# A recommender tower on one core: the fold of Wl ahead of the layers' weights, and 12 of 26 features normalized by ScalarE

## What is computed

```python
e = stack([tbl_f[ids[:, f]] for f in range(26)], axis=1)      # 2048 x 26 x 64
x = layer_norm(dense @ Wd.T, gd, bd)                          # 2048 x 128
y = layer_norm(einsum('bnd,ed->bne', e, Ws), gs, bs)          # each feature to 128 numbers
y = einsum('bne,pn->bep', y, Wsi)                             # 26 features to 32
y = layer_norm(y, gsi, bsi)
T = concatenate([x[:, None, :], swapaxes(y, 1, 2)], axis=1)   # 33 vectors of 128
Z = einsum('bnd,bmd->bnm', T, T)                              # pairwise products
out = layer_norm(Z[:, tril] @ Wl.T, gl, bl) * mask            # 384 of 512 kept
h = relu(concatenate([out, dense], axis=1) @ W_top1 + b_top1)
h = relu(h @ W_top2 + b_top2)
y = h @ W_top3                                                # 2048 x 1
```

## Time and profile before

| | |
|---|---|
| three runs, median (lowest to highest) | 621.14 us (621.01 to 622.87) |
| the profiled execution, in all | 624.07 us |
| its span | 621.9 us |
| TensorE busy, and its mean granted clock | 522.8 us (84%), 0.948 |
| VectorE busy | 518.9 us (83%) |
| ScalarE busy | 295.7 us (48%) |
| GpSimd busy | 403.4 us (65%) |
| gathers on GpSimd | 416, first at 3.14 us, last at 536.09 us |

### The profile page before, as it was taken

How to read it: one execution, slowest core, us unless ns; L and a number is a source line. 1 busy time by engine, 2 the same in 40 slices (tenths; PEclk the granted TensorE clock), 3 DMA queues, 4 the chain that set the end, 5 groups by cost and what they waited for, 6 DMA issues and landing times.

```text
span 621.9 us, 17561 instructions
## 1 busy us (share of the span) xinstructions
PE 522.8 (84%) x6955; PEld 390.4 (63%) x6955; DVE 518.9 (83%) x1073; ACT 295.7 (48%) x730; POOL 403.4 (65%) x422
## 2 busy tenths in 40 slices
PE   1462777689999999999999999999899899988886
PEld 1352555547676767676767676676767577756566
DVE  3499689999999999999998989898989789996610
ACT  0410243545555546464645465555546364635422
POOL 6777775777777777777777777777777777400000
PEclk9955877899999999999999999999999899998999
DMA  7311111111111111111111121111111111100000
GB/s 181 104 25 33 27 29 30 27 35 27 35 29 35 28 37 28 36 27 27 38 27 36 27 38 28 35 29 37 27 38 28 27 27 27 20 1 2 1 1 2
DMA packets 22609, 20.22 MB, mean 33 GB/s; under 512 B 12016, under 2 KB 14720, under 8 KB 22528
## 3 DMA queue, kind: packets, MB, share of 16 engines
q0 software_dynamic: 13312, 13.66, 12.3%
q1 hardware_dynamic: 8400, 4.33, 2.7%
q10 hardware_dynamic: 816, 1.11, 0.6%
HBM read 19.07 MB, written 0.01 MB: 31 GB/s over the span
## 4 chain that ended last, share of the span: by engine, by line
PE 41%; DVE 21%; issue 15%; POOL 9%; ACT 8%; DMA 4%; SPq 2%; ACTq 0%; DVEq 0%; POOLq 0%
POOL emb L255 9%; PE b_y L342 7%; PE b_l L397 7%; PE b_l L414 6%; PE b_l L423 5%; PE b_z L354 4%; DVE nrm L774 3%; DVE V L807 3%; DMA emb<-in_tbl,idx 3%; PE b_mix L330 3%; ACT mixed L501 3%; PE b_a L312 2%; DVE yb L789 2%; DVE byn L784 2%; PE b_a L321 2%
## 5 line engine op out<-in xcount | busy, mean ns | idle before, releaser
L255 POOL DMA_INDIRECT emb<-in_tbl,idx x416 | 402.7, 968 | 132.8 <-issue 117.6
L506 ACT ACTIVATE sq<-yb 128x1024 f32<-128x1024 f32 x64 | 67.7, 1057 | 154.8 <-DVE yb L789 154.8
L789 DVE TENSOR_TENSOR yb<-b_y,bias_y 128x1024 f32<-128x1024 f32 x64 | 78.1, 1220 | 20.3 <-PE b_y L342 19.8
L342 PE MATMUL b_y<-mixed,projw 64*128 64x512 f32 x256 | 74.0, 655 | 24.2 <-ACT mixed L501 24.1
L807 DVE TENSOR_TENSOR V<-yb,rstd_y 128x256 f32<-128x256 f32 x256 | 91.9, 422 | 2.2
L796 DVE TENSOR_REDUCE var_y<-sq 128x32 f32<-128x1024 f32 x64 | 77.8, 1216 | 7.0 <-ACT sq L506 5.6
L397 PE MATMUL b_l<-wlt,zt 128*128 128x512 f32 x160 | 72.9, 602 | 0.8 <-issue 0.8
L330 PE MATMUL b_mix<-mix,byn 128*128 128x128 f32 x512 | 72.3, 287 | 0.0
L321 PE MATMUL b_a<-gram_w,embt 128*128 128x128 f32 x416 | 64.7, 298 | 6.0 <-ACT embt L490 5.2
L490 ACT ACTIVATE embt<-b_a 128x512 f32<-128x512 f32 (+1 forms) x64 | 33.0, 516 | 76.6 <-PE b_a L312 76.5
L354 PEld LDWEIGHTS b_z<-V 128*32 128x32 f32 x4096 | 46.0, 111 | 34.5 <-issue 17.8
(11 more groups left out here) (131 smaller groups left out, 686.8 us busy)
## 6 DMA issues: line engine op xcount, KB each, us to landing
emb<-in_tbl,idx POOLq DMA_INDIRECT x416, 2.5
dense<-in_r_dense_t SPq DMA_DIRECT2D x16, 128.0 KB, 2.2
V<-in_L_rec_Wl ACTq DMA_DIRECT2D x1, 1056.0 KB, 5.2
w<-in_W_top SPq DMA_DIRECT2D x2, 512.0 KB, 6.4
w<-in_W_top SPq DMA_DIRECT2D x1, 768.0 KB, 5.3
out_y<-y_sb SPq DMA_DIRECT2D x16, 0.5 KB
idx<-in_ids SPq DMA_DIRECT2D x1, 195.0 KB, 5.1
wd<-in_L_rec_Wd SPq DMA_DIRECT2D x1, 128.0 KB
```

The costliest lines, as they stand in the source:

```text
L255: pool.indirect_dma_start(out=emb[t % 2][:, f, :], out_offset=None, in_=tables[f], in_offset=bass.IndirectOffsetOnAxis(ap=idx[:, t, f:f + ...
L342: last = nc.tensor.matmul(b_y[:, j2, :], projw[r, :], mixed[c % 2][r, :], start=True, stop=True, tile_position=(64 * j2, 0))
L789: nc.vector.tensor_tensor(yb[c % 2][:, :, :, :].rearrange("e h s p -> e (h s) p"), b_y[:, :, :].rearrange("e h (s p) -> e (h s) p", p=NP), ...
```

## The change

Three things change.

1. W_top1's last two blocks count for `w_mlp` and no longer for `w_x`, and are loaded ahead of W_top2. SyncE waits for `w_wl` ahead of the eight loads of `w_mlp`.
2. Wl's preparation lies earlier: `prepare_wsq` in quarter 0 (ahead of the first variance), `fold` in 1 and 2, `prepare_mlp` and `fold_sums` in 3, `prepare_gain` in 4, `prepare_wlt` in 5 to 9.
3. ScalarE normalizes features 0 to 11, each with one activation with the reciprocal as its scale, in four pieces: 0 to 3 at the end of quarter 4t+3, and in quarter 4t+4 features 4 to 6 ahead of its square, 7 to 9 behind it, and 10 and 11 at the end. VectorE keeps features 12 and 13 of the first half and the second half. A new semaphore `act_nrm` counts the pieces; the shuffle, VectorE's next first half and GpSimd's first batch of a tile wait for it.

```diff
+ACT_FEATURES = 12
+ACT_PIECES = 4
...
-        N_REC, N_X, N_MLP, N_WL = 4, 4, 7, 3
+        N_REC, N_X, N_MLP, N_WL = 4, 3, 8, 3
...
             load(dense[1][:, :], dense_v[1], dense_loaded[1])
+
+            sp.wait_ge(w_wl, 16 * N_WL)
             load(b2[:, :], a["b_top2"].rearrange("(c p) -> p c", p=P), w_mlp, True)
...
+            load(w1[:, 3:5, :], a["W_top1"][MAXD:, :].rearrange("(c p) m -> p c m", p=P), w_mlp)
             load(w2[:, :, :], a["W_top2"].rearrange("(c p) m -> p c m", p=P), w_mlp)
-            load(w1[:, 3:5, :], a["W_top1"][MAXD:, :].rearrange("(c p) m -> p c m", p=P), w_x)
...
                     after(pool, nrm_ready, 2 * (t - 2) + b // 2 + 1)
+                    if b == 0:
+                        after(pool, act_nrm, ACT_PIECES * (t - 1))
...
-                if h == 6:
+                if h == 4:
                     prepare_gain()
-                if 6 <= h < 6 + RC:
-                    prepare_wlt(h - 6)
+                if 5 <= h < 5 + RC:
+                    prepare_wlt(h - 5)
...
+            def normalize(t, lo, hi):
+
+                act.wait_ge(rstdn_done, 2 * t + 1)
+                after(act, byn_ready, 2 * t)
+                for f in range(lo, hi):
+                    last = nc.scalar.activation(nrm[:, :, f], emb[t % 2][:, f, :], ACT.Copy, scale=rstd_n[:, f:f + 1])
+                last.then_inc(act_nrm, 1)
...
+                if (t := tile(h, DENSE_NORM + 1)) is not None:
+                    normalize(t, 4, 7)
...
+                if (t := tile(h, DENSE_NORM + 1)) is not None:
+                    normalize(t, 7, 10)
...
+                if (t := tile(h, DENSE_NORM + 1)) is not None:
+                    normalize(t, 10, 12)
+                if (t := tile(h, DENSE_NORM)) is not None:
+                    normalize(t, 0, 4)
-                if h == 1:
+                if h == 0:
                     prepare_wsq()
...
+                if k == 0:
+                    after(dve, act_nrm, ACT_PIECES * t)
...
-                for f in range(f0, f0 + n, 2):
+                for f in range(max(f0, ACT_FEATURES), f0 + n, 2):
...
                 dve.wait_ge(nrm_ready, 2 * (t + 1))
+                dve.wait_ge(act_nrm, ACT_PIECES * (t + 1))
...
-                if h == 1:
+                if h == 0:
                     prepare_wsq()
-                if h in (2, 3):
-                    fold(h - 2)
-                if h == 4:
+                if h in (1, 2):
+                    fold(h - 1)
+                if h == 3:
                     prepare_mlp()
                     fold_sums()
-                if h == 6:
+                if h == 4:
                     prepare_gain()
-                if 6 <= h < 6 + RC:
-                    prepare_wlt(h - 6)
+                if 5 <= h < 5 + RC:
+                    prepare_wlt(h - 5)
```

More of the change, by code:

```diff
@@ L151, in tower @@
         emb_transposed, embt_copied, gw_done = sem("emb_transposed"), sem("embt_copied"), sem("gw_done")
-        prod_done, varn_done, varm_done, stdn_done, rstdn_done, nrm_ready, byn_ready = (
-            sem("prod_done"), sem("varn_done"), sem("varm_done"), sem("stdn_done"), sem("rstdn_done"), sem("nrm_ready"), sem("byn_ready"))
+        prod_done, varn_done, varm_done, stdn_done, rstdn_done, nrm_ready, act_nrm, byn_ready = (
+            sem("prod_done"), sem("varn_done"), sem("varm_done"), sem("stdn_done"), sem("rstdn_done"), sem("nrm_ready"), sem("act_nrm"), sem("byn_ready"))
         mix_done, mixed_copied, proj_done = sem("mix_done"), sem("mixed_copied"), sem("proj_done")
```

## The result

The changed kernel takes 616.49 us (median of 13 runs, 614.14 to 620.67) beside 622.15 us of the kernel before (13 runs, 619.49 to 625.28). The ratio is 0.9905 with a 95% interval of 0.9887 to 0.9923; times the 621.14 us from above that is 615.2 us, where 615.4 was forecast. It is faster, by 5.7 us. The profiled execution took 615.92 us, its span is 614.1 us (621.9 before), and TensorE's mean granted clock 0.98 (0.948 before). The two clocks are not to be compared: in the start-up this profile shows 1.00 where the matmuls were as slow as before.

The account below looks back on a forecast made before the run. The prediction took GpSimd's gathers as the bound, saturated for 396 us. Removing 4.7 us of its waits and 1.0 us of end lag gives -5.7 us, from 621.14 to 615.4 us; range 612.3 to 618.8.

Parts of the forecast that it names:

- The bound: From 141 us to its last gather GpSimd never waits: saturated for 396 us, at 1.27 us a gather.
- The sum: Over the whole span, GpSimd's vanished waits and less lag at the end give -5.7 us, 621.9 to 616.2.
- -4.7 (waits): GpSimd's real waits for the gram, up to about 141 us, all vanish: 4.7 us, bounds 0 and 4.7.
- -1.0 (lag): Compute behind the gathers at the end: 2.0 us before, 1.0 taken as gained through VectorE's lighter load.
- rival 2: TensorE's clock falls after gather waits: 618 to 622.7 us, about 642 if every tile is hit (under 0.01); 0.11 with another rival.
- The shift that survives is 3.5 us: Start-up: transposes behind the 40th gather, at 61.44 us, can come only 3.5 us earlier, when its data is there.
- It is not on GpSimd's path: VectorE losing 6 of 13 normalizations a tile, 1.5 us a tile, 24 us in all, doesn't delay GpSimd.
- It makes the compute about 30.8 us a tile: VectorE's relief makes compute 30.8 us a tile against GpSimd's 32.8, winning back lag at 2 us a tile, not 0.5.
- Up to 3.6 us a tile: ScalarE's 12 added activations a tile, 302 ns each, cost up to 3.6 us, hidden in its idle time; taken at nothing.
- The rule on the shared port: If VectorE's instructions with two SBUF inputs slow gathers, fewer normalizations save 1.9 us: 613.5 us, left out of the sum.
- the rival's share for nrm: Freer gathers as nrm partly leaves VectorE: 24 of 143.6 us leave, saving 1.9 us; 612.5 to 613.5 us, chance 0.11.
- The rivals on the other side: No earlier start, 620 to 621 us (0.11 with the cold-clock rival); or ScalarE's pieces slow tiles, about 640 us (0.04).

Follow-up runs that it names:

- normalization alone: The changed kernel with loads, copies, folds and Wl's transposition where they were before; ScalarE still normalizes features 0 to 11: 618.14 us beside 621.93, ratio 0.9934.
- start-up part alone: The changed kernel with all 26 features normalized on VectorE again, keeping the changed loads and Wl's earlier preparation: 618.5 us beside 622.87, ratio 0.9933.

## Why the prediction was right, and where its steps were wrong

**The bound: right.** GpSimd's gathers set the time. Where its waits are gone the kernel is 5.7 us shorter, and with 22 gathers a tile it is shorter still, until GpSimd waits again. It is a bound by a narrow margin: 64 gathers fewer, 81 us of GpSimd's time, gave only some 9 us.

**The sum: right in its total, and in its terms only in part.** Forecast for the span was -4.7 (waits) and -1.0 (lag) = -5.7. Measured in the profiled execution: -4.7 waits, -2.2 gathers' own time, -2.1 lag, +1.2 drain = -7.8 (621.9 to 614.1). The medians moved by 5.7. One execution against another thus moved 2 us more than the medians; the execution of before was 2.9 us above the median shown first, so a match to the tenth is partly luck. The scalings that left VectorE are 21.6 us (51.7 to 30.1), not 24. And in rival 2 the sum is wrong: 31 us on top of 615.4 are 646, not 642.

**"The shift that survives is 3.5 us": undersized.** The transposes behind the 40th gather came at 56.22 instead of 61.44, so 5.2 us earlier: that gather ended at 54.6 and not 55.4, and they followed 1.6 us behind it, where I had put the 2.5 us of a usual landing. First shuffle 51.87, forecast 53 or earlier; the last gather started at 529.25, forecast near 531.4. The matmuls of wd came at 10.49, forecast 10.1 to 10.5, and the first batch at 18.92, the late end of the 15.7 to 19 forecast: its last landing took 5.9 us while the weights were loading.

**"It is not on GpSimd's path": wrong in the start-up tiles.** The prediction did add 1.5 us each for tile 0's and the next tile's lighter normalization, but it called VectorE's relief worth only the lag at the end, and the expectations took it that without the start-up part GpSimd's pauses would stay. The normalization alone removes all of GpSimd's waits, the start-up part alone 3.1 of 4.7, and each has a ratio of 0.993; together 0.9905. Both draw on the same 4.7 us, so their gains can't add in full. I had read VectorE's share from the steady tiles and not looked at the tiles from 57 to 157 us, where TensorE has less to do and VectorE is nearly full, in one of them 32.79 of 33.57 us. That either part still adds something to the other is likely but not firm: the intervals are 0.9912 to 0.9955 (start-up part) and 0.991 to 0.9958 (normalization) alone and 0.9887 to 0.9923 together, and they overlap. In the traces with the normalization alone and with both, the 2.6 us of span between them are 1.6 from the gathers, 1.9 from a lag that is a matter of when the cold tile falls, and -1.0 from the drain.

**"It makes the compute about 30.8 us a tile": wrong.** It is 32.15; TensorE's 30.3 us of work and its waits for ScalarE are most of that, and I take them for what sets it. After the cold tile the lag fell by 0.5 to 0.6 us a tile, not by 2. I subtracted VectorE's 1.5 us from a tile that TensorE, at 84% over the span but 94% in these tiles (121.18 of 128.60), was setting. So the lag of 0 at the end isn't VectorE's work: the cold tile fell at tile 7 instead of 14, and eight tiles were left to recover. With the normalization alone it fell at tile 14 again and 1.8 us of lag remained; with the start-up part alone, VectorE at its full load, no tile was cold and no lag remained.

**"Up to 3.6 us a tile" for ScalarE: right in size, and hidden as argued.** By their records the 192 activations took 402 ns in the mean, beside a nearest row of 302; but in a row they overlap, and the group is busy 55.8 us, 0.29 each or 3.5 us a tile. ScalarE keeps 136 us of idle time ahead of its squares. VectorE's reciprocals of the sample side, which wait for ScalarE's root, stood idle 31.2 us; before it was 18.9 us, so part of what VectorE was freed of came back as waiting for ScalarE, on an engine with time to spare.

**The rule on the shared port: half borne out, not settled.** The gathers' mean fell from 968 to 963 ns, 2.2 us in all, close to the 1.9 worked out. By 5.3 ns it just passed the 5 that the prediction had named as a sign of being wrong. But the start-up part alone, with all scalings on VectorE, has 968, the normalization alone, with VectorE as light as in the changed kernel, has 967, and the changed kernel with 22 gathers has 973. The mean doesn't follow nrm. The single gathers in the trace of the kernel before say more: of the 56 that took over 1.0 us, 42 ran beside an instruction that writes `V`, as 93 of all 416 did, and only 10 beside one of nrm, as 62 of all did. So the slow gathers go mostly with V, which stays, and the rival's share for nrm had little ground; what lowered the mean stays open. The Trainium skill ("GPSIMD Engine Reference", Key points) names instructions with two SBUF inputs as what contends with GpSimd; both groups are such, and the trace bears it out for V and not for nrm. Why they differ no run shows.

**The cold TensorE: limited itself, as argued.** One tile in a run is made longer by over 3 us: 36.37 us (tile 14) before, 36.47 (tile 7) after, 35.77 (tile 14) with the normalization alone, none with the start-up part alone. Three stretches of 4 us of the changed kernel, each behind a wait of TensorE for a gather, and one of three tiles in which such waits are short:

```profile
114.14:118.14 4.00, 4.00 (x22) 3.69 (x24) 3.96 (x4) 1.94 (x4) 3.02 (x4) 0.65 0.14 25
147.40:245.79 98.39, 90.77 (x1289) 67.46 (x1287) 86.63 (x162) 61.69 (x165) 74.62 (x79) 1.00 0.17 32
247.30:251.30 4.00, 3.98 (x22) 3.74 (x24) 3.82 (x7) 1.95 (x4) 3.08 (x4) 0.64 0.16 32
81.30:85.30 4.00, 3.96 (x22) 3.84 (x22) 3.93 (x10) 1.91 (x4) 3.06 (x4) 0.59 0.15 27
```

Behind waits of 3.85 (at 81.34), 3.17 and 2.75 us the clock was mostly at its lower level of 1.2 GHz; waits of 0.69 to 1.18 us in between left it at 1.00. The first two fell on tiles in which TensorE has less to do (31.48 and 32.74 us long), so only the third showed. Behind it the compute is late, TensorE doesn't wait, and the clock stays full. The Trainium skill ("TensorE: Matmul & The Clock Gate", HAM oscillation) shows a matmul kernel in which each piece behind a DMA wait of about 3 to 5 us starts cold. The trace agrees for the three long waits; the page does not say it of waits of about 1 us, and the prediction, which left the length out, was wrong that by it each tile would be hit. So rival 2 at its full size had no ground.

**The rivals on the other side** didn't come: 12 activations a tile are no bound, and the earlier start took place.

## What to carry to other kernels

When the chain of waits shows little of an engine, still ask of it what it waits for; one that waits for nothing over hundreds of us sets the pace there. An engine's relief is worth what it is worth in each stretch by itself: the same 1.5 us a tile was worth nothing in the steady tiles (32.3 us a tile before and after), and 1.3 us in the early tile in which TensorE has less to do and Wl's preparation fills VectorE. And two changes that each remove the same wait must be tried one at a time, since their gains can't add in full.

## What the runs showed of the hardware that was not expected

- The same program takes 622 us on some chips and 794 to 803 on others. For the start-up part alone there is a profile of either kind. The gathers cost the same (970 and 968 ns), and the granted clock was 0.92 beside 0.98. On the slower chip TensorE stops 138 times, 100.8 us in all, inside runs of 64 small matmuls (once, for 1.0 us, on the other), and in the start-up several engines stand still for 5 to 10 us with no releaser in this kernel's program ("remote" in the two lines below, VectorE's and ScalarE's): the first shuffle came at 90.86 us and not at 52.92. What causes it no run shows.
- ScalarE's strided activations of 128x64 take 402 ns each by their records, but overlap to 0.29 us apiece in a row.

```profile
41.02 0.27 DVE L707 MEMSET wex<- 128x256 f32 x1 [8.98 <-remote]
```

```profile
74.55 0.49 ACT L495 ACTIVATE embt<-b_a 128x384 f32<-128x384 f32 x1 [9.51 <-remote]
```
